# The per-query shift of a transformer's softmax: its two bfloat16 parts kept in the words of the negative maximum, and its rows placed by part instead of by half

## The reference

```python
attn = jnp.einsum('blhd,bmhd->bhlm', Q, K) * scale     # per batch and head: 128 x 128
attn = jax.nn.softmax(attn, axis=-1)                   # over the keys
out = jnp.einsum('bhlm,bmhd->blhd', attn, V)
```

## Time and profile before

| what | value |
|---|---|
| timed runs, median of three | 1096.98 us (1094.63 to 1103.36) |
| profiled execution, span of its instructions | 1087.7 us |
| TensorE busy | 973.1 us, 89% |
| VectorE busy | 855.0 us, 79% |
| ScalarE busy | 692.1 us, 64% |
| GpSimd busy | 649.3 us, 60% |
| mean granted TensorE clock | 0.958 of full |

### The profile page before, as it was taken

How to read it: one execution, slowest core, us unless ns; L and a number is a source line. 1 busy time by engine, 2 the same in 40 slices (tenths; PEclk the granted TensorE clock), 3 DMA queues, 4 the chain that set the end, 5 groups by cost and what they waited for, 6 DMA issues and landing times.

```text
span 1087.7 us, 33962 instructions
## 1 busy us (share of the span) xinstructions
PE 973.1 (89%) x10494; PEld 694.1 (64%) x10494; DVE 855.0 (79%) x2398; ACT 692.1 (64%) x1801; POOL 649.3 (60%) x1020
## 2 busy tenths in 40 slices
PE   3699999989998888999998889889999999768997
PEld 2466666656665667777776677665656655556885
DVE  6588899888888778888887888776787877657665
ACT  1377777777776743555665887673666666546775
POOL 8757778877676466640675786168667752323443
PEclk9599999999998979999998999998999999989999
DMA  5776567985666201332332111035555640054551
GB/s 147 181 148 132 116 139 163 185 162 134 143 153 171 74 34 50 98 105 77 106 104 55 37 31 38 26 64 133 115 113 129 130 106 18 6 196 167 194 193 29
DMA packets 81460, 119.69 MB, mean 110 GB/s; under 512 B 16720, under 2 KB 62704, under 8 KB 80288
## 3 DMA queue, kind: packets, MB, share of 16 engines
q1 hardware_dynamic: 66704, 85.24, 32.9%
q0 software_dynamic: 9472, 27.27, 8.2%
q10 hardware_dynamic: 5136, 5.31, 2.5%
HBM read 80.75 MB, written 36.18 MB: 107 GB/s over the span
## 4 chain that ended last, share of the span: by engine, by line
PE 61%; DVE 19%; issue 8%; DMA 5%; ACT 3%; POOL 3%; SPq 1%; DVEq 0%; POOLq 0%; ACTq 0%
PE heads_ps_pv L992 4%; PE heads_ps_max L970 4%; DVE heads_neg_max L770 4%; PE cross_ps_max L960 4%; PE experts_ps_gu L2488 4%; PE cross_ps_max L970 3%; PE cross_ps_pv L992 3%; DMA QK<-heads_qk_parts 2%; PE experts_ps_gu L2490 2%; PE experts_ps_gu L2489 2%; PE heads_ps_out L1054 2%; PE experts_ps_y L2509 2%; PE experts_ps_y L2510 2%; PE experts_ps_hT L2496 1%; PE cross_ps_qk L1316 1%
## 5 line engine op out<-in xcount | busy, mean ns | idle before, releaser
L770 DVE TENSOR_REDUCE heads_neg_max<-heads_ps_max 128x4 f32<-128x512 f32 x256 | 169.5, 681 | 36.0 <-PE heads_ps_max L970 34.4
L844 ACT ACTIVATE heads_E<-heads_ps_exp 128x512 f32<-128x512 f32 x256 | 150.1, 603 | 22.1 <-PE heads_ps_pv L992 17.3
L970 PE MATMUL heads_ps_max<-QK 48*128 48x128 bf16 x1024 | 102.9, 226 | 10.2 <-DMA QK<-heads_qk_parts 5.8
L770 DVE TENSOR_REDUCE cross_neg_max<-cross_ps_max 128x4 f32<-128x512 f32 x128 | 86.2, 682 | 29.5 <-PE cross_ps_max L970 28.9
L974 PE MATMUL heads_ps_exp<-QK 50*128 50x128 bf16 x1024 | 103.0, 222 | 0.0
L2182 POOL DMA_INDIRECT experts_gathered<-experts_y_dram,experts_index x64 | 62.0, 969 | 65.4 <-DMA experts_y_dram<-experts_y_sb 44.1
L844 ACT ACTIVATE cross_E<-cross_ps_exp 128x512 f32<-128x512 f32 x128 | 76.5, 599 | 33.1 <-PE cross_ps_exp L974 17.0
L2404 ACT ACTIVATE experts_act_out<-experts_ps_gu 128x256 f32<-128x256 f32 x110 | 42.3, 384 | 83.0 <-PE experts_ps_gu L2490 82.9
L970 PEld LDWEIGHTS heads_ps_max<-QK 48*128 48x128 bf16 x1024 | 58.9, 97 | 52.2 <-issue 21.0
L1613 POOL TENSOR_TENSOR experts_hidden_lo<-experts_hidden,experts_hidden_hi 128x512 fp32r<-128x512 f32 x32 | 41.4, 1293 | 73.9 <-ACT experts_hidden_hi L1837 66.8
L992 PE MATMUL heads_ps_pv<-heads_E,heads_V 128*32 128x128 f32 x2048 | 84.8, 285 | 0.0
(11 more groups left out here) (325 smaller groups left out, 3173.3 us busy)
## 6 DMA issues: line engine op xcount, KB each, us to landing
experts_share<-experts_cT_dram SPq DMA_DIRECT2D x7, 2304.0 KB, 8.8
heads_qk_parts<-heads_parts POOLq DMA_DIRECT2D x32, 384.0 KB, 4.7
QK<-heads_qk_parts SPq DMA_DIRECT2D x64, 192.0 KB
QK<-heads_qk_parts SPq DMA_DIRECT2D x64, 128.0 KB
cross_qk_parts<-cross_parts POOLq DMA_DIRECT2D x16, 384.0 KB, 4.2
QK<-cross_qk_parts SPq DMA_DIRECT2D x32, 192.0 KB
experts_xs_dram<-load_stats SPq DMA_DIRECT2D x26, 192.0 KB, 3.0
experts_xs<-experts_xs_dram SPq DMA_DIRECT2D x78, 64.0 KB
```

What stands on the lines that cost most here:

```text
L770: nc.vector.tensor_reduce(neg_max[:, half, heads.start:heads.stop], ps_max[:, u % 2, :].rearrange("q (h k) -> q h k", h=HU), AX.X, ALU.max ...
L844: nc.scalar.activation(E[:, half, heads.start:heads.stop, :], ps_exp[:, u % 2, :].rearrange("k (h q) -> k h q", h=HU), ACT.Exp, scale=scal ...
L970: last_max = nc.tensor.matmul(ps_max[:, u % 2, i * S:(i + 1) * S], QK[q_of][rows, 0, h, max_of], QK[q_of][rows, 1, h, max_of], start=not m ...
```

## The change

The tile shift goes, and neg_max becomes two buffers, used by batches in turn. A float32 word of neg_max is seen as two bfloat16 values: its high half is the value cut off after bfloat16's bits, and that is now the high part, without any instruction. One VectorE instruction subtracts it from the whole word and writes the result, as bfloat16, over the word's low half. The transpose reads the words themselves, so the order of the 32 rows changes from (half, part, head) to (half, head, part). The transfers follow: instead of one per half with both parts, there is one per part with both halves; its source is every second row of shiftT and its destination two partitions that lie 64 apart. The high part is cut off instead of rounded; the low part takes up the difference.

The waits change with it. Ahead of the first maximum VectorE waits for the transpose of two batches before (shiftT_made) in place of the subtract of the batch before; ahead of the subtract only the wait for the four maxima is left.

```diff
-        neg_max = sb("neg_max", [S, HALVES, HH])
-        shift = sb("shift", [S, HALVES, SHIFT, HH], BF16)
+        neg_max = [sb(f"neg_max{p}", [S, HALVES, HH]) for p in range(2)]
...
-        shift_hi = sem("shift_hi")
...
+        def shift_of(t, ahead):
+
+            return neg_max[(t.k + ahead) % 2][:].rearrange("q a h -> q (a h)").bitcast(BF16).rearrange("q (a h i) -> q a h i", a=HALVES, i=SHIFT)
...
-                    for half in range(HALVES):
-                        at = half * BASE + ROWS
-                        sp.dma_start(QK[p][at:at + SHIFT, 0, :, j * S:j * S + S], turned[half * SHIFT * HH:(half + 1) * SHIFT * HH, :]).then_inc(shift_placed[(t.k + MA - 1) % 2], 16)
+                    for i in range(SHIFT):
+                        at = ROWS + i
+                        sp.dma_start(QK[p][at:at + BASE + 1:BASE, 0, :, j * S:j * S + S], turned[i:SHIFT * H:SHIFT, :]).then_inc(shift_placed[(t.k + MA - 1) % 2], 16)
...
                     if u == 0:
-                        need(dve, shift_ready, t.batch(1, MA))
+                        need(dve, shiftT_made, t.batch(1, MA - 1))
                     half, heads = heads_of(u)
-                    nc.vector.tensor_reduce(neg_max[:, half, heads.start:heads.stop], ps_max[:, u % 2, :].rearrange("q (h k) -> q h k", h=HU),
+                    nc.vector.tensor_reduce(neg_max[(t.k + MA) % 2][:, half, heads.start:heads.stop], ps_max[:, u % 2, :].rearrange("q (h k) -> q h k", h=HU),
...
                     dve.wait_ge(max_taken, t.batch(UNITS, (MA + 1) * UNITS))
-                    need(dve, shiftT_made, t.batch(1, MA))
-                    nc.vector.tensor_copy(shift[:, :, 0, :], neg_max[:]).then_inc(shift_hi, 1)
-                    dve.wait_ge(shift_hi, t.batch(1, MA + 1))
-                    nc.vector.tensor_tensor(shift[:, :, 1, :], neg_max[:], shift[:, :, 0, :], ALU.subtract).then_inc(shift_ready, 1)
+                    low, high = (shift_of(t, MA)[:, :, :, i] for i in range(SHIFT))
+                    nc.vector.tensor_tensor(low, neg_max[(t.k + MA) % 2][:], high, ALU.subtract).then_inc(shift_ready, 1)
...
-                nc.tensor.transpose(ps_shiftT, shift[:].rearrange("q a i h -> q (a i h)"), identb[:]).then_inc(shiftT_made, 1)
+                nc.tensor.transpose(ps_shiftT, shift_of(t, MA - 1).rearrange("q a h i -> q (a h i)"), identb[:]).then_inc(shiftT_made, 1)
```

## The result

The changed kernel took 1084.83 us (median of 15 runs, 1073.2 to 1099.25) beside 1094.39 us for the kernel before (15 runs): the ratio is 0.9874, 95% interval 0.9844 to 0.9905. The prediction was 1087 us, 10 us less than before. The same kernel was measured four more times beside the experiments, with ratios of 0.9929 [0.9894, 0.9964], 0.9919 [0.9884, 0.9953], 0.9917 [0.9874, 0.9960] and 0.9934 [0.9897, 0.9971]. So the change brings 0.7 to 1.3% by these ratios, 7 to 14 us, and 7 to 9 us in four of the five measurements.

What follows compares the result with a forecast made beforehand. The prediction took TensorE's wait for the shift in the first layers' loop with VectorE as the bound: 8.7 us there plus 1.3 for the maxima gave 10.0, from 1096.98 to 1087 us, its own range 1083 to 1092.

Steps and rivals of the forecast that it cites:

- What bounds the kernel: First two attention layers: TensorE's shift transpose waits for the subtract 27 times, 11.2 us, in a loop through both engines.
- The instruction removed: VectorE's cast goes: shift ready 0.21 us earlier in each of 96 batches; the remaining subtract takes 175 ns.
- The neighbours: GpSimd's instructions holding VectorE's subtract: it escapes them from 142 to 200 us, is held like the cast from 243 to 318.
- The split into 0.21 us and holding: From 142 to 200 us, 4.0 us of gain counted as 2.3 by the cast's absence and 1.7 by escaping GpSimd.
- The sum at the transpose: TensorE's waits for the shift, 11.2 us: 8.7 us go, as 4.0, 0.8, 1.3 by stretch and 1.3 plus 1.3 at the ends.
- the ends: Start-up and last batches of the first layers: 4.0 us in 6 waits, of which 1.3 and 1.3 us go.
- The maxima: Matmuls' waits for a maximum, 2.7 us in 8 waits: half goes, 1.3 us.
- The transfers there stay where they are.: From 200 to 243 us the 2.8 us of waits for the parts' transfer stay unchanged, while 0.8 us goes.
- the parts' transfer ends the wait instead: From 200 to 243 us, in the rival where time is taken back: gain 0 to 5 us, 1094.5 us, chance 0.24.
- The waits, the buffer, the transfers: VectorE's new wait on the transpose of two batches ago, the second buffer and the changed row transfers cost or gain 0.
- The masked layer: Near 740 to 916 us TensorE is full and hides the saving; the layer stays as long as it was.
- everything opens up: Rival: escape from GpSimd in all stretches, all 11.2 and 2.7 us of waits vanish; gain 16.6 us, 1080 us, chance 0.15.

Runs made afterwards that it cites:

- copy_ahead: Changed kernel with a cast to an unused tile and its semaphore wait put back ahead of the subtract; ratio to the kernel before 0.9992.
- reduce_behind: Changed kernel with an extra reduction of 16 finished words right behind the subtract, without a wait of its own; ratio to the kernel before 0.9876.
- after_again: Changed kernel measured again with no edit, first repetition, whose profile is used; ratio to the kernel before 0.9929.
- reduce_ahead: Changed kernel with a reduction of the same 16 words and its wait ahead of the subtract; ratio to the kernel before 0.9999.
- rows_only: Kernel before, keeping its cast and subtract, with a tile laid out by (half, head, part) and the new transfers by part; ratio to before 0.9989.
- low_left_out: Changed kernel without the low part's transfer in the first layers' 64 batches, rows of ones instead; ratio to the kernel before 0.9856.
- copy_behind: Changed kernel with the cast behind the subtract and a wait on each side of it; ratio to the kernel before 1.0142.
- after_fifth: Changed kernel measured again with no edit, beside the kernel with the parts' transfers first in odd steps; ratio to the kernel before 0.9934.
- after_third: Changed kernel measured again with no edit, a further repetition; ratio to the kernel before 0.9919.

## Why the prediction was right

The predicted drop of 10.0 us stands beside 9.6 us between the medians, 13.8 us by the first ratio (1.26% of 1094.39) and 7 to 9 us by the four repetitions. The time and the sign were right, and so was the place. The terms were right to differing degrees, and that the total came out so close is in part luck: terms too small and a term left at nothing made up for each other.

- *What bounds the kernel.* Right. The shift's transpose was the place: copy_ahead takes the whole gain away with one instruction ahead of it, and reduce_behind leaves it with an instruction of the same length behind it.
- *The instruction removed.* 0.21 us earlier, and duration unchanged: 179 ns for 175 taken. Right.
- *The neighbours.* From 142 to 200 us the subtract slips ahead of L686 and L692 as foreseen, and a batch takes 4.73 us for "some 4.7". For 243 to 318 us I said that it would be held as the cast was, and that only 1.3 of 1.5 us would go. That step failed in the safe direction: in after_again 3 of the 15 subtracts there are held, and no wait of TensorE for the shift is left; why the stretch settled in another rhythm isn't shown. And from the earlier trace rows I concluded wrongly that L683 doesn't hold a cast. The mean of 235 ns lies in the 200 to 270 named. The split into 0.21 us and holding was a mistake of kind, as reduce_ahead showed.
- *The sum at the transpose.* 8.7 us of 11.2 were to go; 9.5 went (11.2 − 1.7). By the starts of the subtracts the gain lies elsewhere than my sum had it: from 142 to 200 us a batch takes 4.73 for 5.01 us, 3.4 us in 12 (4.0 forecast); from 200 to 243 us 4.99 for 5.25, some 2 us in 8 (0.8); from 243 to 318 us 4.76 for 5.02, some 4 us in 15 (1.3). Also, the 4.0 us in 6 waits that I gave to the ends lay there only for 2.7 us in 3 waits; 1.3 us in 3 waits stood from 58 to 142 us.
- *The maxima.* Half of 2.7 us was to go: 1.2 went in after_again, and 0.2 to 0.8 in the other profiles. Too high.
- *"The transfers there stay where they are."* This term was mis-sized, and it is the one that counts. Waits for the parts rose from 5.2 to 12.5 us, 7.3 of the 9.5 won at the transpose; the other profiles have 11.7 to 14.5. Of before there is one profile only: rows_only, copy_ahead and reduce_ahead, which have no gain, show 7.0, 7.5 and 6.8, so some 5 us of the rise may be the change's. I had this only as a rival ("the parts' transfer ends the wait instead") and for 200 to 243 us alone. They now stand in every stretch up to 318 us. That faster batches ask for the same transfers sooner is the likely reason, not one shown apart; that SP's queue is part of it, low_left_out suggests.
- *The waits, the buffer, the transfers.* 0, and measured so: rows_only 0.9989, copy_ahead 0.9992. That the new transfers issue 0.11 us sooner each was not foreseen. It shows in no time while TensorE waits for the shift; whether it helps in the changed kernel, where SP's queue is part of the bound, wasn't tried.
- *The masked layer* was to stay as long. It took 170.5 us for 174.1. But copy_ahead, which has no gain, took 171.2 and reduce_ahead 170.9. The granted clock from 740 to 920 us was 0.98 in before, rows_only and copy_behind (174.0 to 174.1 us) and 1.00 in after_again, copy_ahead and reduce_ahead, so nearly all of it is the clock and not the change.

How can 9.5 us less here and 5 to 7 more there give 9 us? By stages the first layers took 305.0 us for 316.8 in after_again, 11.8 us less, and 305.7 in after_fifth, though 315.7 in after_third, where the clock was lower. The busy table of that whole stage, for before and for after_fifth, which stood at nearly the same granted clock there (0.96 and 0.97), says where the time lay (columns of the earlier trace rows, before first):

```profile
37.70:354.50 316.80, 291.04 (x4589) 191.60 (x4587) 273.85 (x732) 229.63 (x555) 229.17 (x403) 0.96 0.70 152
```

```profile
37.70:343.30 305.60, 283.13 (x4589) 189.69 (x4587) 256.14 (x668) 228.08 (x555) 228.46 (x403) 0.97 0.75 158
```

With the same 4589 matmuls TensorE was idle for 22.5 us where it had been for 25.8, only 3.3 us less, and busy for 7.9 us less. The view of waits has 17.9 us in 25 waits for 22.1 in 46. So a list of waits shows less than half of what the stage gained; the rest stood in TensorE's busy time. The ends of matmuls are modelled in these rows, so it is likely that each wait also hides some loss behind the matmul ahead of it. By this division that would be 7.9 / 21, some 0.4 us a wait, an estimate. The prediction had such a term, 0.1 us a wait, in its rival "everything opens up" and not in its own sum.

What the stages add is a give-back outside the attention: the time between the first layers' last shift and the masked layer's first was 388.6 us before and 396.3 in after_again. There the granted clock fell to 0.5 and 0.7 in two slices; from 355 to 420 us it was 0.70 on the mean, against 0.84 before. copy_ahead (0.74) and reduce_ahead (0.63) have the low clock too, without any gain, and rows_only (0.89) has not. With one profile of each, I can't say that the change causes it. But the mean clock of every execution is on record. In the four repetitions it was 0.9571 over 46 executions of the changed kernel and 0.9615 over 95 of before beside them, a difference of 0.0044 with a standard error of 0.0019, and within either kernel an execution with 0.01 less clock took some 3.2 us longer. So on the mean execution a lower clock gives back some 1.4 us, an estimate, and not the 8 us that these two profiles differ by. Whether the change is its cause stays open.

## What to carry to other kernels

In a loop that runs through two engines, an instruction counts by what waits behind it, not by its length. A reduction of some 0.17 us on VectorE, which GpSimd can't hold, cost the whole gain of 0.7 to 1.3% ahead of the transpose, with the wait that follows it, and nothing behind the subtract, with none. So look for the row of waits that names the instruction's result before counting instructions. Where a short instruction's mean is far over its median, ask which instruction of another engine it meets, and expect that moving it by its own length changes who is met. And when such a wait goes, read the second line of the same list: here the parts' transfers took over part of it at once, and neither of two reorderings of their queue won it back, because the wait for one transfer was traded for that for another.

## What the hardware showed that I had not expected

- The issue of a transfer on SP took 510 ns with 16 source partitions two apart and two destination partitions 64 apart, and 619 ns with 16 adjacent ones and two adjacent ones, at the same 4 KB. Which side makes the difference wasn't tried.
- A cast or subtract on VectorE that was held beside one of GpSimd's arithmetic instructions ended 0.02 to 0.05 us behind that instruction, whatever was left of it. Where about 0.1 us was left of it, nothing was lost: 16 casts beside L683 took their usual 0.17 us.
- Of two VectorE instructions in a row, of which GpSimd can hold the first or the second, the holding passes to the second when the first is exempt: 176 to 179 ns for the reduction, a median of 364 for the subtract behind it.
- A 16-element write to every second half-word took 4 ns more than a dense one (178 against 174 at least, in rows_only, and the same in place in after_again).
